# Scan layers of an audio tower: states kept in PSUM, rows spread by DMA, sums on TensorE

## The chip, the cores and the metric

The kernel runs on one core of one Trainium2 chip. The metric is the device time of one execution in microseconds. Everything is float32.

## The reference

The input `x` is 32 sequences of 750 tokens with 64 channels. Three state-space layers run one after the other; after each of the first two, pairs of neighbouring tokens are averaged (750, 375, 187 tokens). Then come a Taylor-softmax attention block and a block of 16 experts with top-2 gates, each on a layer norm and with a residual. The change touches the three scan layers alone:

```
A = -exp(A_log)                                  # 64 channels x 64 states
dbc = x @ W_dbc.T                                # per token: one delta, B (64), C (64)
delta = softplus(delta * W_dt + b_dt)            # per token and channel
dA  = exp(delta * A);  dBx = delta * x * B
h[t] = dA[t] * h[t-1] + dBx[t]                   # for each channel and state
y = sum over states of h * C  +  D * x
```

With the inputs' `A_log` (large), nearly all states decay to zero within one token. For them `h = dBx`, and their whole sum is a quadratic form of `x` times `delta * x`.

## The kernel before

Channels of two halves of the batch lie on the 128 partitions. A **unit** is 750 columns of tokens (748 in the third layer); there are 28: 16 in the first layer, 8 in the second, 4 in the third. Units are grouped in eight **phases** (`PHASES`): 4, 4, 4, 4, 4, 4, 2, 2 units. For each phase a **decision** is made from the data: the extremes of the raw delta (`extreme_rows`, eight matmuls into one pair of PSUM banks), the smallest delta, the states that are not "fast", their ranks, the matrix `mT2` of the fast states' quadratic form, and the two **slots** (`STATIC = 2`) of slow states that are scanned one after the other. `more_slots` is a branch for further ones, which these inputs do not take. Decisions of phases 1 to 6 are spread over the units q = 0, 1, 2 of the phase ahead (`chain`); those of phases 0 and 7 are made in one go (`straight`, before unit 0 and in the period of unit 24).

Each engine runs `period(n)`, a fixed order written out by hand, for n from -2 to 27, and meets the others by semaphores. Per unit:

- TensorE (PE), in calls of `wide` (one matmul of 512 columns and one of 238): `z` (raw delta on all partitions), `mixed` (the quadratic form's matrix times x), `summed` (sum over channels of a product), `weighted_b` for slots 0 and 1 (B spread over the partitions), `weighted_c` for slots 0 and 1 (C likewise): 7 wide calls.
- ScalarE (ACT): `softplus` of unit n+2 in five passes over `pairs[0]`, `decay` (exp) for each slot.
- GpSimd (POOL): `summed` and `corrected` (two adds that finish delta), `inputs` (`u = delta * x`), `pool_output` (pairs of tokens of `y0T` added), `add` for each slot (pairs of tokens added, then added to the next layer's x).
- VectorE (DVE): `load` (B times u, in place in PSUM) for 2 slots, `recur` (the scan, PSUM to SBUF) for 2 slots, `read` (state times C) for 2 slots, `product`, `by_delta`, `output`, `corrected`: 10 passes of 750.
- SyncE (SP) loads x in seven parts, then the later parameters (`later`, 15 transfers), and in the scans nothing else.

After the last unit attention and experts start; they wait for the last `add`.

## Time and profile before

| | |
|---|---|
| three runs | 847.52 us median (841.94 to 850.53) |
| profiled execution | 842.01 us, span 840.2 us, mean TensorE clock 0.959 |
| first scan starts / scans end / attention starts | 44.60 / 369.0 / 371.87 us |
| busy in the span | PE 738.7, DVE 569.5, POOL 482.3, ACT 364.2 us |

A busy PE is not PE at its peak: matmul ends are modelled. A line can be that of a helper: all wide matmuls have lines 388 and 389, and the tiles tell them apart. A record of a float32 matmul comes twice (x2). In the scans the start of one instruction to the start of the next (its **pitch**) is shorter than its duration, since neighbours overlap.

### The profile page before, as it was taken

The page shows a single profiled execution, that of the slowest core. Times are in us where ns is not written, and L with a number is a line of the kernel's source. Part 1 is how long each engine was busy: PE and PEld are TensorE (multiplying, and loading weights), DVE is VectorE, ACT ScalarE, POOL GpSimd, SP SyncE. Part 2 cuts the span into 40 slices and gives each one's busy share as a digit, 9 for nine tenths or more (in the row PEclk, how much of TensorE's full clock was granted, in tenths as well). Part 3 has the DMA queues.
Part 4 walks back from the last instruction along what each step waited for, and adds up shares of the span by engine and source line. Part 5 has one row for each costly group of instructions (what it writes and reads, how often), then busy time and mean ns, then how long its engine had stood idle before and what let it go on. Part 6 is the DMA issues. An engine that isn't in the chain of part 4 may idle for free.

```text
span 840.2 us, 10716 instructions
## 1 busy us (share of the span) xinstructions
PE 738.7 (88%) x3396; PEld 383.1 (46%) x3396; DVE 569.5 (68%) x861; ACT 364.2 (43%) x638; POOL 482.3 (57%) x508
## 2 busy tenths in 40 slices
PE   4689888998889896855998888979999999999997
PEld 2345454554545453522776666753333333333332
DVE  3199899999999997665348888848454445444443
ACT  2345555454655454312444444444344333443332
POOL 2379788988888896543555555523344434444441
PEclk9699999999999999776799999999999999999999
DMA  8200000000000000022000000063594433444400
GB/s 300 80 1 1 1 1 2 0 2 1 2 1 1 2 0 1 1 55 45 2 1 1 3 4 3 3 126 78 106 188 89 91 88 84 98 98 98 104 1 19
DMA packets 19078, 37.40 MB, mean 45 GB/s; under 512 B 2255, under 2 KB 17607, under 8 KB 18375
## 3 DMA queue, kind: packets, MB, share of 16 engines
q1 hardware_dynamic: 18711, 36.01, 18.5%
q8 instruction: 30, 0.49, 0.2%
q10 hardware_dynamic: 304, 0.63, 0.2%
q14 instruction: 33, 0.27, 0.1%
HBM read 34.72 MB, written 1.92 MB: 44 GB/s over the span
## 4 chain that ended last, share of the span: by engine, by line
PE 66%; DVE 16%; ACT 7%; issue 5%; POOL 1%; DVEq 0%; ACTq 0%; POOLq 0%
PE pair L712 21%; PE pair L388 12%; PE pair L733 10%; PE pair L389 5%; PE pair L615 5%; DVE tmp L1107 4%; PE pair L598 3%; PE pair L647 2%; ACT work L776 2%; ACT work L777 2%; DVE pair L1080 1%; PE pair L445 1%; PE pair L634 1%; PE pair L477 1%; DVE tmp L1115 1%
## 5 line engine op out<-in xcount | busy, mean ns | idle before, releaser
L1360 DVE TENSOR_TENSOR hidden<-pair,tmp 128x502 f32<-128x502 f32 (+1 forms) x192 | 121.5, 675 | 130.1 <-PE pair L712 105.2
L1520 POOL TENSOR_TENSOR hidden<-xs,big 128x502 f32<-128x502 f32 (+1 forms) x96 | 111.8, 1166 | 167.4 <-PE pair L712 146.5
L964 ACT ACTIVATE tmp<-pair 128x502 f32<-128x502 f32 (+1 forms) x192 | 102.5, 586 | 156.9 <-PE pair L712 156.9
L1544 POOL TENSOR_TENSOR big<-big 94x512 f32<-94x512 f32 (+3 forms) x120 | 89.6, 782 | 81.4 <-DVE big L1262 71.7
L712 PE MATMUL pair<-xs,w 64*128 64x502 f32 (+1 forms) x384 | 108.2, 640 | 0.5 <-DVE big L1294 0.5
L712 PE MATMUL pair<-hidden,w 64*128 64x502 f32 (+1 forms) x384 | 98.6, 589 | 1.8 <-DVE hidden L1360 1.6
L1107 DVE TENSOR_TENSOR_SCAN tmp<-tmp,pair 128x750 f32<-128x750 f32 (+1 forms) x56 | 95.5, 1705 | 0.1
L733 PE MATMUL pair<-hidden,w 128*64 128x502 f32 (+1 forms) x384 | 91.1, 596 | 0.0
L794 ACT ACTIVATE tmp<-big,picked 128x749 f32<-128x749 f32 (+2 forms) x56 | 51.1, 912 | 86.6 <-issue 49.5
L388 PE MATMUL pair<-big,work 128*128 128x512 f32 x128 | 67.5, 609 | 11.8 <-ACT work L777 3.6
L1382 POOL TENSOR_TENSOR big<-big,work 128x750 f32<-128x750 f32 (+1 forms) x28 | 45.5, 1624 | 48.5 <-ACT big L781 48.5
L388 PE MATMUL pair<-x,work 128*128 128x512 f32 x96 | 51.7, 621 | 11.9 <-DVE tmp L1115 3.9
L712 PEld LDWEIGHTS pair<-xs,w 64*128 64x128 f32 x384 | 29.6, 187 | 67.3 <-issue 36.0
L712 PEld LDWEIGHTS pair<-hidden,w 64*128 64x128 f32 x384 | 37.3, 189 | 48.8 <-issue 46.0
L1097 DVE TENSOR_TENSOR pair<-pair,big 128x750 f32<-128x750 f32 (+1 forms) x56 | 52.2, 931 | 2.2 <-issue 2.0
L1389 POOL TENSOR_TENSOR big<-big,work 128x750 f32<-128x750 f32 (+1 forms) x28 | 46.5, 1662 | 10.3 <-DVE work L1067 8.6
L1115 DVE TENSOR_TENSOR tmp<-tmp,pair 128x750 f32<-128x750 f32 (+1 forms) x56 | 51.7, 924 | 0.5 <-PE pair L389 0.4
L733 PEld LDWEIGHTS pair<-hidden,w 128*64 128x64 f32 x384 | 23.4, 136 | 61.9 <-DVE hidden L1360 34.8
L1414 POOL TENSOR_TENSOR x<-x,work 128x375 f32<-128x375 f32 (+1 forms) x48 | 43.8, 913 | 6.9
L776 ACT ACTIVATE work<-pair,packed 128x750 f32<-128x750 f32 (+1 forms) x28 | 24.8, 886 | 47.4 <-PE pair L389 47.4
L615 PEld LDWEIGHTS pair<-big 93*120 93x120 f32 (+1 forms) x384 | 42.8, 186 | 2.6 <-issue 1.4
L615 PE MATMUL pair<-big 93*120 93x65 f32 (+1 forms) x384 | 43.3, 270 | 0.0
(187 smaller groups left out, 1265.7 us busy)
## 6 DMA issues: line engine op xcount, KB each, us to landing
big<-dispatched SPq DMA_DIRECT2D x40, 502.0 KB, 6.6
big<-in_x SPq DMA_DIRECT2D x3, 1500.0 KB, 11.8
big<-dispatched SPq DMA_DIRECT2D x8, 498.0 KB, 5.8
w<-in_w SPq DMA_DIRECT2D x5, 512.0 KB, 7.1
big<-in_x SPq DMA_DIRECT2D x4, 375.0 KB, 4.0
out<-resid SPq DMA_DIRECT2D x8, 187.0 KB, 7.6
packed<-in_packed ACTq DMA_DIRECT2D x1, 424.5 KB, 4.7
dispatched<-tmp SPq DMA_DIRECT2D x8, 47.0 KB, 1.5
```

Of the source, the lines that this page charges most:

```text
L388: pe.matmul(dst[:, 0:512], lhsT, rhs[:, 0:512], start=True, stop=True)
L615: mm = pe.matmul(bank[4 + n % 2][0:FT, at:at + 65], kF[r % 2][0:rows, unit, FT * f:FT * f + FT], qkv[r % 2][0:rows, unit, 143:208], start= ...
L712: pe.matmul(dst[:, 0:hi - lo], weights[blk, HID * e:HID * e + HID], x[blk, :], start=True, stop=True)\
L733: mm = pe.matmul(bank[4][64 * b:64 * b + 64, 0:hi - lo], w3[:, e, :], hidT[(2 * expert + b) % 8][:, 0:hi - lo], start=(e == 0), stop=(e == ...
L794: act.activation(seqs(dA[j], l)[:, :, 1:], seqs(of(delta, n), l)[:, :, 1:], ACT.Exp, scale=picked[p % 2][:, j:j + 1]).then_inc(dk_a, 1)
L964: act.activation(sT[i % 4][:, 0:w], bank[BANK1[i]][:, 0:w], ACT.Silu).then_inc(silu_a, 1)
L1097: v.tensor_tensor(bu, bu, of(u, n), ALU.mult).then_inc(bu_v, 1)
L1107: v.tensor_tensor_scan(hT[j][:, 0:w], dA[j][:, 0:w], pairs[j][:, 0:w], 0.0, ALU.mult, ALU.add)\
L1115: v.tensor_tensor(h, h, pairs[2][:, 0:w], ALU.mult).then_inc(hc_v, 1)
L1360: v.tensor_tensor(hidT[i % 8][:, 0:hi - lo], bank[BANK2[i]][:, 0:hi - lo], sT[i % 4][:, 0:hi - lo], ALU.mult)\
L1520: pool.tensor_tensor(xw[e % 4][:, 0:hi - lo], xs[:, lo:hi], wx[:, e, 0:hi - lo], ALU.mult)\
L1544: ins = eng.tensor_tensor(dst[:, :, at:at + H * m].rearrange("p u (h d) -> p u h d", d=m), t[:, :, :, 0:m], t[:, :, :, k:D], ALU.mult)
```

## The change

- **States in PSUM.** `recur` scans in place over B u in `pairs[1]` and `pairs[2]`; `read` writes state times C to SBUF (`hC`, double).
- **Rows spread by DMA.** `z` and `weighted_c` go. In their place `rows(k)` makes, with four 32-column matmuls in one bank, the two slots' rows of C (unit n+1) and the raw delta's row (unit n+3); ACT copies them to SBUF (`rows_out`), and SP writes them to DRAM (4 transfers) and reads them back spread over 64 partitions each (2 transfers for delta, `St`; 2 for C, `Ct`).
- **Sums on TensorE.** `sums(n, part)` adds D x and both slots' parts for even and odd tokens in one bank: six matmuls of 375 (374) columns; ACT copies the sum to the next layer's x (`sums_out`); POOL adds the fast states' part (`add`, once a unit).
- **Softplus.** The scaling by `W_dt` is ACT's (`wdtc`); the correction, once a DVE pass, is a sixth ACT pass and one more POOL pass. ACT does `softplus` in two parts.
- `by_delta` and `output` become one DVE pass (times `u`). The decisions' POOL steps go to ACT and DVE.
- Buffers: delta and u are rings of 7 units; x parts 4 to 6 and `later` are issued between the first events.

The diff, cut:

```diff
+RING = 7
+LATE_Z = UB[NP - 1] - 2
+ROWS = {-2: [(None, 0), (None, 1)]}
+for _n in range(-1, UNITS - 1):
+    ROWS[_n] = [(_n + 1, _n + 3 if _n + 3 < UB[NP - 1] else None)]
+    if _n == LATE_Z:
+        ROWS[_n] = [(_n + 1, UB[NP - 1]), (None, UB[NP - 1] + 1)]
@@ SyncE @@
+            def spread_rows(k):
+                i, written = k % 2, 16 * sum(2 for e in EVENTS[:k + 1] for m in e if m is not None)
+                sp.wait_ge(rw_a, k + 1)
+                if k > 1:
+                    landed(k - 2)
+                for m, row, at, count in zip(EVENTS[k], (0, 4), (0, 64), (4, 2)):
+                    if m is not None:
+                        half = unit(m)[2] // 2
+                        for c in range(2):
+                            sp.dma_start(rowsd[i, row:row + count, half * c:half * c + half],
+                                         rowsT[i][at + 32 * c:at + 32 * c + count, 0:half]).then_inc(rw_d, 16)
+                sp.wait_ge(rw_d, written)
...
-            for i in range(1, 7):
+            for i in range(1, 4):
                 load(i)
-            sp.wait_ge(zeroed, 1)
-            for dst, src in later:
-                sp.dma_start(dst, src).then_inc(later_in, 16)
-            sp.wait_ge(xa_g, STATIC * UNITS)
+            for k in range(len(EVENTS)):
+                spread_rows(k)
+                if k in (1, 2, 3):
+                    load(k + 3)
+                elif k == 4:
+                    sp.wait_ge(zeroed, 1)
+                    for dst, src in later:
+                        sp.dma_start(dst, src).then_inc(later_in, 16)
+            sp.wait_ge(xa_g, UNITS)
@@ TensorE @@
+            def sums(n, part):
+                terms = [(diagD[:, l, :], x)] + [(ident, t) for t in hC[n % 2]]
+                    if part == 0:
+                        after(pe, sm_a, TAKEN[n] - 1)
+                    pe.wait_ge(hc_v, STATIC * n + part + 1)
+                    for i in ((0, 1), (2,))[part]:
+                        for k, t in enumerate(halves(terms[i][1], l)):
+                            mm = pe.matmul(parts(bank[1], l), terms[i][0], t, start=(i == 0 and k == 0),
+                                           stop=(i == 2 and k == 1))
...
              def period(n):
+                if q == 1:
+                    extremes_spread(p)
                 if here:
                     weighted_b(n, 1)
+                if q in (1, 2):
+                    pe.wait_ge(dec_v, p * DECV + (3, 8)[q - 1])
+                for k in range(EVENT_AT[n], EVENT_AT[n + 1]):
+                    rows(k)
+                old = n - 1 if n > 0 and last_of(n - 1) is None else None
...
+                if old is not None:
+                    sums(old, 0)
+                if nxt:
                     summed(n + 1)
...
+                if nxt and q != 0:
+                    weighted_b(n + 1, 0)
+                if old is not None:
+                    sums(old, 1)
+                if q == 0:
+                    pe.wait_ge(dec_v, p * DECV + 1)
+                    weighted_b(n + 1, 0)
                 if n + 2 < UNITS:
-                    z(n + 2)
+                    mixed(n + 2)
...
                 if last_of(n) is not None:
+                    sums(n, 0)
+                    sums(n, 1)
                     more_slots(last_of(n))
...
 @@ ScalarE @@
             def period(n):
+                if n >= 0:
+                    decay(n, 1)
+                if q == 1:
+                    bounds(p)
+                for k in range(EVENT_AT[n], EVENT_AT[n + 1]):
+                    rows_out(k)
+                if nxt and s is not None:
+                    decay(n + 1, 0)
+                if n + 2 < UNITS:
+                    softplus(n + 2, 0)
+                if q == 1:
+                    exponents(p)
+                if n + 2 < UNITS:
+                    softplus(n + 2, 1)
+                if old is not None:
+                    sums_out(old, 0)
+                if nxt and s is None:
+                    decay(n + 1, 0)
...
+                if s is not None:
+                    bounds(s)
...
 @@ VectorE @@
             def recur(n, j):
+                h = pairs[1 + j][:, 0:w]
+                v.tensor_tensor_scan(h, dA[j][:, 0:w], h, 0.0, ALU.mult, ALU.add).then_inc(sc_v, 1)
             def read(n, j):
+                v.wait_ge(c_d[n % 2], 32 * (n // 2 + 1))
+                v.tensor_tensor(hC[n % 2][j][:, 0:w], pairs[1 + j][:, 0:w], Ct[n % 2][:, j, 0:w], ALU.mult)
...
 @@ GpSimd @@
             def period(n):
                 if 0 <= n + 1 < UNITS:
-                    corrected(n + 1)
+                    softplus(n + 1)
+                    inputs(n + 1)
                 if n > 0:
-                    add(n - 1, 1)
+                    add(n - 1)
```

## Rows read from the trace of the kernel before

**Rows 1.** Busy time by stage: length, PE, PEld, DVE, ACT, POOL (instructions), PEclk, DMA, GB/s.

```profile
91.50:137.80 46.30, 41.20 (x146) 22.93 (x145) 43.00 (x50) 24.54 (x35) 39.33 (x41) 1.00 0.00 1
276.40:322.10 45.70, 40.64 (x138) 22.73 (x137) 42.55 (x51) 24.72 (x37) 39.88 (x41) 1.00 0.01 1
322.10:343.30 21.20, 14.98 (x51) 8.46 (x50) 12.23 (x21) 7.59 (x14) 14.28 (x16) 0.80 0.00 0
343.30:371.80 28.50, 20.59 (x59) 10.82 (x58) 24.75 (x24) 7.55 (x9) 14.83 (x9) 0.92 0.00 1
...
370.00:842.00 472.00, 431.70 (x2352) 212.80 (x2352) 260.98 (x487) 187.82 (x377) 203.42 (x221) 0.96 0.29 62
```

**Rows 2.** VectorE timeline of one unit: start us, us, engine, line, operation, [idle <-releaser].

```profile
172.88 1.70 DVE L1107 TENSOR_TENSOR_SCAN tmp<-tmp,pair 128x750 f32<-128x750 f32 x1
174.50 0.92 DVE L1097 TENSOR_TENSOR pair<-pair,big 128x750 f32<-128x750 f32 x1
175.33 0.92 DVE L1115 TENSOR_TENSOR tmp<-tmp,pair 128x750 f32<-128x750 f32 x1
...
181.11 0.94 DVE L1067 SCALAR_TENSOR_TENSOR work<-pair,work 128x750 f32<-128x750 f32 x1 [0.65 <-ACT pair L783]
182.50 0.95 DVE L1097 TENSOR_TENSOR pair<-pair,big 128x750 f32<-128x750 f32 x1 [0.45 <-issue]
...
184.20 1.70 DVE L1107 TENSOR_TENSOR_SCAN tmp<-tmp,pair 128x750 f32<-128x750 f32 x1
```

**Rows 3.** TensorE timeline, two `wide` calls in a row.

```profile
137.45 1.02 PE L388 MATMUL pair<-big,work 128*128 128x512 f32 x2
...
138.71 1.02 PE L388 MATMUL pair<-work,packed 128*128 128x512 f32 x2
```

**Rows 4.** TensorE timeline, the eight 32-column matmuls of `extreme_rows`.

```profile
189.52 1.47 PE L445 MATMUL pair<-x,w0pm 128*32 128x375 f32 x16 [0.36 <-ACT work L777]
```

**Rows 5.** Instruction groups of ACT and POOL, 91.5 to 322 us: count | busy, mean ns.

```profile
L1414 POOL TENSOR_TENSOR x<-x,work 128x375 f32<-128x375 f32 (+1 forms) x40 | 36.7, 917 | 5.7
L794 ACT ACTIVATE tmp<-big,picked 128x749 f32<-128x749 f32 (+2 forms) x40 | 36.5, 912 | 59.0 <-issue 32.9 <-DVE tmp L1107 22.1 <-DVEq L1138 4.0
...
L1382 POOL TENSOR_TENSOR big<-big,work 128x750 f32<-128x750 f32 (+1 forms) x20 | 32.6, 1630 | 14.9 <-ACT big L781 14.9
...
L1394 POOL TENSOR_TENSOR big<-big 128x750 f32<-128x750 f32 x11 | 19.9, 1809 | 0.0
...
L776 ACT ACTIVATE work<-pair,packed 128x750 f32<-128x750 f32 (+1 forms) x20 | 17.7, 887 | 26.8 <-PE pair L389 26.8
```

**Rows 6.** DMA: issue ns min/median/max; GB/s, 600 to 640 us; KB each, us to landing.

```profile
L359 SPq DMA_DIRECT2D big<-dispatched x48: 573/613/676, 553.2 to 779.1; - x48
...
GB/s 213 213 217 197 225 197 215 205 195 223 199 219 213 195 223 199 237 193 199 231 199 225 201 60 6 14 269 219 209 215 102 0 0 0 0 0 12 275 215 221
...
big<-in_x SPq DMA_DIRECT2D x3, 1500.0 KB, 11.8
...
dispatched<-tmp SPq DMA_DIRECT2D x8, 47.0 KB, 1.5
```

**Rows 7.** Timeline of the two decisions made in one go, at 21 and 332 us.

```profile
21.55 0.16 DVE L1044 TENSOR_REDUCE low<-pair 128x1 f32<-128x2 f32 x1 [0.68 <-PE pair L455]
...
332.30 0.16 DVE L1044 TENSOR_REDUCE low<-pair 128x1 f32<-128x2 f32 x1 [0.47 <-PE pair L455]
...
339.10 0.36 DVE L1060 COPY picked<-pair 128x192 f32<-128x192 f32 x1 [1.70 <-PE pair L477]
...
339.51 2.07 PE L388 MATMUL pair<-x,quad 128*128 128x512 f32 x2 [0.45 <-DVE picked L1060]
```

**Rows 8.** GpSimd timeline, the last sum of the scans.

```profile
370.13 1.63 POOL L1417 TENSOR_TENSOR resid<-resid,tmp 128x748 f32<-128x748 f32 x1 [0.97 <-DVE tmp L1115]
```

**Rows 9.** SyncE timeline, first and last of 15 issues of `later`.

```profile
9.25 0.57 SPq L337 DMA_DIRECT2D wqkv<-in_wqkv  x1
...
22.20 0.35 SPq L337 DMA_DIRECT2D w<-in_w  x1
```

More of the change, by code:

```diff
@@ L85, in program @@
         tmp = sb("tmp", [128, 3256])
-        delta = [big[:, 12000 + 3000 * i:15000 + 3000 * i] for i in range(2)]
-        u = [big[:, 18000 + 3000 * i:21000 + 3000 * i] for i in range(2)]
+        delta, u = (big[:, at:at + 750 * RING] for at in (13500, 18750))
         packed = sb("packed", [128, PACKED])
@@ L118, in program @@
         sext = sb("sext", [1, 2])
-        nz, zb, rz, dmin, dn, de, dL = (sb(f"low{i}", [128, 1]) for i in range(7))
+        nz, rz, dmin, dn, de, dL = (sb(f"low{i}", [128, 1]) for i in range(6))
         amax2 = sb("amax2", [128, NS])
@@ L476, in picks @@
+            def picks(p):
+                l = PHASES[p][0]
+                pe.wait_ge(dec_v, p * DECV + 9)
                 for i, t in enumerate((AT, wBT, wCT)):
-                    mm = pe.matmul(pairs[pair][:, NS * i:NS * i + NS], t[:, l, :], onehot[:, :], start=True, stop=True)
+                    mm = pe.matmul(bank[0][:, NS * i:NS * i + NS], t[:, l, :], onehot[:, :], start=True, stop=True)
                 mm.then_inc(dec_p, 1)
@@ L759, in _ @@
             mm.then_inc(setup_p, 1)
+            pe.wait_ge(setup_v, 2)
+            for l in range(LAYERS):
+                mm = pe.matmul(bank[4][:, l:l + 1], wdtr[0:1, l, :], ident[0:1, 0:1], start=True, stop=True)
+            mm.then_inc(setup_p, 1)
             pe.wait_ge(setup_v, SETUP_V)
+            pe.wait_ge(zeroed, 2)
             for n in range(-2, UNITS):
@@ L1151, in period @@
                     load(n, 1)
+                if q == 1:
+                    smallest_delta(p)
+                if here:
                     read(n, 0)
[L1153 to L1155 removed]
                     recur(n, 1)
+                if q == 0:
+                    extremes(p)
+                elif q == 1:
+                    classes(p)
+                elif q == 2:
+                    picks(p)
                 if nxt:
                     output(n + 1)
[L1159 to L1164 removed]
                 if here:
@@ L1375, in _, with softplus @@
             pool.sem_inc(more_g, 1)
-            def summed(n):
+            def softplus(n):
                 _, _, w, _ = unit(n)
-                d = of(delta, n)
+                d, e = of(delta, n), E[n % 2][:, 0:w]
                 pool.wait_ge(log_a, n + 1)
```

538 lines of the change are left out of this document (263 added, 275 removed).

## Prediction

> **What bounds the kernel now.** I read the busy time by stage first. The scan stage runs in phases of four units that repeat at 46 us; VectorE is busy 43.0 of 46.3, TensorE 41.2, GpSimd 39.3, ScalarE 24.5 [rows 1]. The stage from 370 us on (472 us) holds nothing that the change touches, so its cost is carried over. Then VectorE's own timeline: a scan has a pitch of 1.62 us, another pass of 750 columns 0.83 to 0.86 (I take 0.84). Ten passes are 2 x 1.62 + 8 x 0.85 = 10.0 us; the unit shown, in which no step of a decision falls on VectorE, takes 184.20 - 172.88 = 11.32, and the gaps are a wait for ScalarE (0.65) and a branch at the phase's end (0.45) [rows 2]. So VectorE sets the pace.
>
> TensorE's busy time hides how near it is. Two wide calls in a row start 1.26 us apart: 1.68 ns a column [rows 3]. Seven of them are 8.8 us a unit, 35.3 a phase. The eight 32-column matmuls of `extreme_rows` take 1.47 together [rows 4]: 3000 columns at 0.49 ns, so four column groups run at once. Busy 41.2 less 35.3 and 1.5 leaves at most 4.4 for the decision's small matmuls; records overlap, and I take 2.7. TensorE's real load is 39.5 of 46.3, with 6.8 idle.
>
> **The change, part by part**, in a phase of four units of layers 1 and 2.
>
> *VectorE* loses `corrected` and one of `by_delta`/`output`; the scan writes PSUM instead of SBUF, and no row has that. Passes in place in PSUM (0.92) and SBUF to SBUF through PSUM (0.92) cost alike [rows 2], so I take 1.62; bounds 1.5 and 1.8. Eight passes are 2 x 1.62 + 6 x 0.84 = 8.3 us: 1.7 us a unit saved, if VectorE stays the bound. The decision's steps that come over from GpSimd (a few small passes, some 1 us a phase) lie in the slack that this leaves; if VectorE were the bound they would cost that 1 us.
>
> *TensorE* loses three wide calls (-3.78). It gains `rows`, four 32-column matmuls of 375 columns in four groups, half of `extreme_rows`: 0.74. And it gains `sums`, six matmuls of 375 full-width columns: 6 x 375 x 1.68 ns = 3.78. A unit is 4 x 1.26 + 0.74 + 3.78 = 9.56 us; a phase 38.2 + 1.5 + 2.7 = 42.4, against 39.5. **TensorE becomes the bound.** Laid out by hand from `weighted_b(n, 1)` at 0: rows to 2.0, sums 0 to 4.5, `summed` to 5.8, `weighted_b(n+1, 0)` to 7.1, sums 1 to 8.3, `mixed` to 9.6. VectorE's 8.3 us fits in with some 0.8 to spare before `mixed` and `weighted_b(n+1, 1)`. The last unit of a phase carries two units' sums and the branch (13.9), q = 0 none. TensorE's stalls: q = 0 waits for the reduction of the extremes (1.1) and their row (0.35), the branch costs 0.5, q = 1 waits for `fast_weights` behind ScalarE's queue (0.6), q = 2 for the ranks (0.3): 2.8. A phase is 45.2; bounds 42.4 (no stall) and 49.2 (as much idle as now). Against 46.1 that is -0.9 a phase, -5 over the five phases to 322 us.
>
> The sums read every second token. No row shows a matmul that does; the bounds are 1.68 ns a column and twice that, +15 us a phase. GpSimd adds 375 such pairs (`add`) without any penalty, which speaks for the lower end, and I take it. The Trainium skill ("SBUF — State Buffer", the block on cachelines) says that a step of up to four fp32 is free, and no run here shows it for TensorE.
>
> *GpSimd* per unit: three passes for delta (1.63 each), `inputs` 1.81, one add in halves (0.8) and one of 0.92 [rows 5]: 8.4, under 9.6. But `add(n-1)` now waits for TensorE's sums and ScalarE's copy, and stands ahead of the next softplus. From the sums' end at 8.5: copy 0.6, add 1.0, three passes and `inputs` 6.9, `output` 0.85, then `mixed`: 2 units in 19.4 us, so 9.7 a unit. It binds about with TensorE and has no slack.
>
> *ScalarE*: six passes at a pitch of 0.8, two decays of 0.91 [rows 5], two half-width copies of 0.5: 7.6 us a unit. It stays hidden.
>
> *The DMA round trip* is new. SP issues eight transfers a unit: a small one 0.3 to 0.6, a spread one 0.61 [rows 6]. From `weighted_b` at 0: rows out at 2.8, writes issued to 4.7, landed at 5.8 (1.5 for a small one), spread reads issued to 8.3. They move 384 KB (delta) and 768 KB (C); spreads run at some 210 GB/s [rows 6], so 5.5 us and C is there at 13.3. `read(n+1, 0)` wants it at 13.5 to 14.5: hidden, by 0.2 to 1.2. If that cover is gone, each late us costs about half a us a unit. The Trainium skill ("DMA: Bandwidth & Descriptors", Anatomy of one DMA) gives 2.0 us of fixed cost, heaviest for writes to HBM; this trace's 1.5 for a small write speaks for less. By 2.0 the write lands 0.5 later and half of the cover is gone, which would speak for the second rival below.
>
> *Start.* ScalarE's `bounds` of the first decision now stands behind `softplus(0)`, which waits for a round trip: delta's minimum is known at 21.55 [rows 7], softplus ends at some 25.4, so the decision is 3.8 late. Against this, unit 1's softplus needs no z by then. I get the first scan at 43.5 to 45 (44.6 now): 0. In phase 0, x parts 5 and 6 (1500 KB each) and then `later` go between events on one queue. The 15 issues of `later` take 22.55 - 9.25 = 13.3 us [rows 9], 5.4 of it one blocked issue; with 8.3 the event of unit 3 is some 3 us late. Phase 0 would save 0.6 and loses 3 and 1.6 (first C): +4. Bounds 0 and +12.
>
> *The straight decision at unit 24.* The stage from scan 24 to scan 25 is 21.2 us at a granted clock of 0.80 [rows 1]: 10.2 to the minimum, 6.8 to the picks, then a wide call at the lower clock (2.07 for 512 columns, 1.02 elsewhere) [rows 3, 7]. After: `bounds(s)` stands behind `softplus(26, ...)`, and row 26 leaves only in this period: `weighted_b` 2.5 us behind the scan, rows and copy 2.7, writes and landing 2.8, delta spread 3.5, softplus 4.9, `bounds` 1.0: 17.4, then 6.1 to the picks. `weighted_b(25, 0)` comes behind them, ahead of `mixed`, both on a slow clock: 6.3 instead of 4.2 to the next scan. 29.8, so **+8.6**; bounds +3 and +12.
>
> *Tail* (28.5 now [rows 1]). Two units of sums, 3.8 us each, stand where VectorE has no `product` to hide them, and the last unit's come behind the last read: 3.8, copy 0.6, add 1.63 [rows 8], where only the add was. I get 33.6, **+5.1**; bounds +3 and +8.
>
> **Sum**: 0 + 4 - 5 + 8.6 + 5.1 = +12.7; I halve the first phase's +4, since C's wait overlaps the late event: +10. The profiled execution took 842.0, so 852. It is at the low end of its runs (median 847.5); I leave the forecast at **853**.
>
> **Rivals.** *Faster*: TensorE fills its gaps, a phase costs 42.8, and the straight decision loses 4 only. 5 x -3.3, -3 in phase 0, +4, +4: -11.5, about 831. For it: the decision's waits are short and TensorE's queue is in order but never starved by VectorE (8.3 under 9.6). Against: GpSimd's loop of 9.7. It decides from a phase under 44.
> *Slower by a wait*: C lands 3 us later than laid out (17 instead of 13.3), since transfers with others queued land late: 1500 KB of x took 11.8 us [rows 6], and the eight issues of an event share one queue. The loop C, read, `weighted_b(n+1, 0)`, sums 1, `mixed`, next `weighted_b` is (18.1 + 3)/2 = 10.6 a unit: +20 over the scans, 873. It decides from 1.3 us of lateness.
> *Strided sums at half rate*: +3.8 a unit, some 950.
>
> **Chances.** My layout (843 to 863) 0.52; faster rival 0.23; wait rival 0.20; strided 0.05. Within 1% (about what tells from no change here, 8.5 us): 0.36 of the first, 0.04 of the second. Slower: 0.16 of the first, and the last two. The range, 831 to 877, takes in the bounds of the phase (42.4 to 47 for most).
>
> **What would show it.** TensorE's start-to-start over a whole phase and its idle: 45 us with under 3 idle and VectorE near 37 busy of 45. `read` waiting for DMA `spread` says the round trip binds. A 375-column matmul of `sums` at 0.63 pitch; four of `rows` in 0.74. Scan 25 starting 30 us behind scan 24, with ScalarE's first bound at 17. The end of the last add 4 us later behind the last read. A phase above 47 or under 44 would prove my layout wrong.

## The result and the profile after

| | before | after |
|---|---|---|
| median of the runs shown | 847.3 us (841.9 to 850.5, 4 runs) | 873.6 us (863.8 to 875.3, 4 runs) |
| ratio, 95% interval | | 1.029 [1.020, 1.039] |
| profiled execution, span | 842.0, 840.2 us | 875.3, 873.5 us |
| first scan starts | 44.6 | 42.7 |
| attention starts | 371.9 | 398.9 |

The change made the kernel 2.9% slower. 853 had been forecast, with a range to 877; the likeliest case's own range ended at 863, so the total is that of the rival by a wait (873), though not by its mechanism: that the range still holds the result is luck. Where the scans lose their 27.1 us, by the starts of the first slot's scans (a phase is four units; all us; the column of the prediction adds up to +11.2, where its own sum rounds the five phases to -5 and the whole to +10):

| stretch | before | after | difference | predicted |
|---|---|---|---|---|
| start to first scan, and phase 0 | 44.6 + 46.9 | 42.7 + 49.0 | +0.2 | +2 |
| phases 1, 2, 3 | 46.3, 46.4, 46.0 | 46.1, 46.0, 46.1 | -0.5 | -2.7 |
| phase 4 (units 16 to 19) | 46.2 | 49.3 | +3.1 | -0.9 |
| phase 5 (units 20 to 23) | 45.7 | 48.3 | +2.6 | -0.9 |
| scan 24 to scan 25 (straight decision) | 21.2 | 34.8 | +13.6 | +8.6 |
| scan 25 to attention (tail) | 28.6 | 36.6 | +8.0 | +5.1 |

The profile after, by stage, answers to [rows 1]: length, PE, PEld, DVE, ACT, POOL (instructions), PEclk, DMA, GB/s.

```profile
42.70:91.70 49.00, 41.05 (x157) 21.03 (x158) 37.03 (x45) 32.32 (x51) 29.19 (x22) 0.97 0.67 190
91.70:137.80 46.10, 44.72 (x179) 23.41 (x178) 36.92 (x47) 32.77 (x50) 32.99 (x25) 1.00 0.40 105
229.90:279.20 49.30, 45.98 (x179) 23.63 (x178) 37.11 (x46) 32.88 (x51) 32.84 (x25) 0.97 0.38 95
279.20:327.50 48.30, 45.77 (x167) 23.87 (x166) 36.49 (x46) 32.85 (x51) 32.87 (x25) 0.96 0.35 92
327.50:362.30 34.80, 20.96 (x66) 10.38 (x65) 11.65 (x22) 11.89 (x23) 14.38 (x10) 0.71 0.18 45
362.30:398.90 36.60, 27.72 (x86) 14.01 (x85) 22.09 (x21) 13.12 (x20) 13.24 (x8) 1.00 0.18 43
398.90:873.50 474.60, 437.34 (x2352) 217.34 (x2352) 261.34 (x486) 187.70 (x377) 201.72 (x220) 0.95 0.29 61
```

In the second row VectorE fell from 43.0 to 36.9 and TensorE rose from 41.2 to 44.7 of 46.1: the bound changed hands and the pace did not move. Phases 4 and 5 have the same matmuls as that row or fewer (179 and 167), a lower granted clock, and take 3.2 and 2.2 us more. The last row is the untouched stage. Before, the same stretch reads:

```profile
371.90:840.20 468.30, 431.67 (x2352) 212.74 (x2352) 260.92 (x486) 187.82 (x377) 201.71 (x220) 0.96 0.29 62
```

The same 2352 matmuls take 5.7 us more TensorE time and the stage 6.3 more, at a mean granted clock of 0.95 instead of 0.96; the other engines' busy time agrees within 0.5 us. That is where this pair's other 6.3 us lie (with the 27.1, and but for rounding, the 33.3 between the spans). Nothing in that stage was changed, and the medians differ by 26.3 us, so I count it as the clock of these two executions and not as a cost of the change. The experiments below bear this out: none of them touches the stage, and it took from 463.5 us (clock 0.98) to 473.7 us (0.95) in their profiles. Totals of single runs can differ by 10 us from this alone, so the stages are what to compare.

**One unit after** (TensorE's timeline of unit 11; start us, us, engine, line, operation).

```profile
172.81 1.02 PE L454 MATMUL pair<-big,work 128*128 128x512 f32 x2
...
174.17 0.51 PE L476 MATMUL pair<-big,rowsel 128*32 128x375 f32 x2
...
174.93 1.59 PE L514 MATMUL pair<-big,diagD 128*128 128x375 f32 x4
...
177.68 1.02 PE L454 MATMUL pair<-work,packed 128*128 128x512 f32 x2
178.53 0.56 PE L455 MATMUL pair<-work,packed 128*128 128x238 f32 x2
178.94 1.02 PE L454 MATMUL pair<-big,work 128*128 128x512 f32 x2
...
180.20 1.50 PE L514 MATMUL pair<-tmp,packed 128*128 128x375 f32 x4
181.53 1.02 PE L454 MATMUL pair<-big,quad 128*128 128x512 f32 x2
182.39 0.57 PE L455 MATMUL pair<-big,quad 128*128 128x238 f32 x2
182.79 1.48 PE L514 MATMUL pair<-big,diagD 128*128 128x375 f32 x4
```

The order is the one laid out by hand: `weighted_b`, `rows`, `sums` part 0, `summed`, `weighted_b`, `sums` part 1, `mixed`. There is no wait in it. Start to start: 1.36 + 0.76 + 2.75 + 1.26 + 1.26 + 1.33 + 1.26 = 9.98 us, where I had 9.56. VectorE in the same stretch:

```profile
173.01 0.94 DVE L1227 TENSOR_TENSOR work<-pair,big 128x750 f32<-128x750 f32 x1 [1.14 <-PE pair L455]
173.87 1.72 DVE L1249 TENSOR_TENSOR_SCAN pair<-tmp,pair 128x750 f32<-128x750 f32 x1
175.49 0.92 DVE L1242 TENSOR_TENSOR pair<-pair,big 128x750 f32<-128x750 f32 x1
...
180.01 0.94 DVE L1235 TENSOR_TENSOR work<-pair,big 128x750 f32<-128x750 f32 x1 [1.13 <-PE pair L455]
```

Now it is VectorE that waits for TensorE. A scan in place in PSUM starts 1.62 us before the next pass, as the scan to SBUF did [rows 2].

**The new waits of phase 4.** GpSimd, then TensorE:

```profile
234.47 1.78 POOL L1536 TENSOR_TENSOR big<-big 128x750 f32<-128x750 f32 x1
...
237.10 0.98 POOL L1548 TENSOR_TENSOR big<-big,work 128x375 f32<-128x375 f32 x1
```
```profile
235.92 0.56 PE L455 MATMUL pair<-work,packed 128*128 128x238 f32 x2
238.44 2.73 PE L532 MATMUL pair<-big,w0pm 128*32 128x375 f32 x16 [1.95 <-POOLq L1572]
```

`extreme_rows` for phase 5 reads x of the second layer, whose last quarter holds the sums of units 14 and 15. GpSimd's `add(15)` stands at the end of its period, behind softplus and `inputs`, and the branch behind it. TensorE waits 1.95 us, and then the eight 32-column matmuls take 2.73 where they took 1.47 [rows 4]: the granted clock is 0.50 there (238.4 to 241.2).

**The straight decision.** TensorE, then ScalarE:

```profile
331.80 0.82 PE L476 MATMUL pair<-big,rowsel 128*32 128x374 f32 x4
335.61 0.82 PE L482 MATMUL pair<-big,w0pm 128*32 128x374 f32 x4 [2.99 <-POOL big L1548]
...
350.53 0.42 PE L547 MATMUL pair<-packed,amax 128*64 128x128 f32 x1 [6.20 <-ACT amax L907]
...
356.10 2.07 PE L454 MATMUL pair<-big,work 128*128 128x512 f32 x2 [0.45 <-DVE picked L1221]
```
```profile
343.80 1.01 ACT L868 ACTIVATE work<-spread,packed,wdtc 128x748 f32<-128x748 f32 x1 [4.20 <-DMA spread<-rowsd]
...
348.86 0.28 ACT L898 ACTIVATE low<-low,packed 128x1 f32<-128x1 f32 x1
```

Read from the end: the picks are at 355.7, 28.2 us behind scan 24 (327.5; [rows 7] for before). ScalarE's first bound starts at 348.86, right behind the softplus of unit 26, which waited 4.20 for delta's rows by DMA. Those rows left late, since the matmuls for them (L482) waited 2.99 us for a late `add` again, that of unit 23. All the while the delta's minimum, all that the bound needs, was there at 344.5.

**The tail** (TensorE, the last unit):

```profile
391.71 0.87 PE L522 MATMUL pair<-big,diagD 128*128 128x374 f32 x2 [1.64 <-DVE work L1259]
392.42 1.42 PE L522 MATMUL pair<-work,packed 128*128 128x374 f32 x4
394.41 0.90 PE L522 MATMUL pair<-big,diagD 128*128 128x374 f32 x2 [0.57 <-ACT resid L937]
395.14 1.42 PE L522 MATMUL pair<-work,packed 128*128 128x374 f32 x4
398.96 1.59 PE L653 MATMUL pair<-resid,centering 128*128 128x376 f32 x2 [2.39 <-POOL resid L1551]
```

Behind the last read (its end: 391.57) stand two halves of three matmuls in one bank, with ScalarE's copy between them (0.57 wait), the second copy (396.60) and the add (397.22 to 398.85): 7.3 us. In the third layer the change takes the sum in two parts that share `bank[1]`.

### The profile page after: what moved, and what is told of

Same layout as the page of the kernel before. It is cut to its first block, busy times and chain, and to the rows that moved or that the text cites. A ratio compares the mean times of both kernels' runs of the same rounds, so it can differ in the third digit from the quotient of the medians.

```text
span 873.5 us, 11316 instructions
## 1 busy us (share of the span) xinstructions
PE 778.2 (89%) x3626; PEld 393.0 (45%) x3626; DVE 529.6 (61%) x841; ACT 426.2 (49%) x753; POOL 435.1 (50%) x399
## 3 DMA queue, kind: packets, MB, share of 16 engines
q1 hardware_dynamic: 28855, 68.76, 32.4%
## 4 chain that ended last, share of the span: by engine, by line
PE 44%; DVE 7%; ACT 2%; issue 1%; POOL 0%; POOLq 0%; DVEq 0%; ACTq 0%
PE pair L798 20%; PE pair L819 10%; PE pair L701 5%; PE pair L684 3%; PE pair L733 2%; PE pair L720 1%; DVE big L1341 1%; PE pair L748 1%; PE pair L742 1%; PE pair L665 1%; PE pair L522 0%; DVE big L1346 0%; DVE big L1359 0%; DVE big L1636 0%; ACT big L1057 0%
## 5 line engine op out<-in xcount | busy, mean ns | idle before, releaser
L1249 DVE TENSOR_TENSOR_SCAN pair<-tmp,pair 128x750 f32<-128x750 f32 (+1 forms) x56 | 95.8, 1710 | 1.2 <-ACT tmp L892 1.1
L454 PE MATMUL pair<-big,work 128*128 128x512 f32 x112 | 61.2, 628 | 11.6 <-DVE smx L1184 5.3
L1548 POOL TENSOR_TENSOR big<-big,work 128x375 f32<-128x375 f32 (+1 forms) x24 | 22.0, 915 | 81.2 <-ACT big L937 80.7
L819 PEld LDWEIGHTS pair<-hidden,w 128*64 128x64 f32 x384 | 23.4, 136 | 61.9 <-DVE hidden L1504 34.8
L701 PEld LDWEIGHTS pair<-big 93*120 93x120 f32 (+1 forms) x384 | 47.1, 202 | 3.3 <-issue 2.2
L1536 POOL TENSOR_TENSOR big<-big 128x750 f32<-128x750 f32 (+1 forms) x28 | 46.6, 1665 | 2.2
L701 PE MATMUL pair<-big 93*120 93x65 f32 (+1 forms) x384 | 47.4, 285 | 0.0
L1531 POOL TENSOR_TENSOR big<-big,work 128x750 f32<-128x750 f32 (+1 forms) x28 | 46.2, 1649 | 2.2
L1529 POOL TENSOR_TENSOR work<-work 128x750 f32<-128x750 f32 (+1 forms) x28 | 46.3, 1652 | 0.8 <-ACT work L881 0.8
L733 PE MATMUL pair<-big 120*64 120x188 f32 x384 | 37.4, 347 | 1.9 <-issue 1.2
```

The lines of the kernel that those rows point to most:

```text
L454: pe.matmul(dst[:, 0:512], lhsT, rhs[:, 0:512], start=True, stop=True)
L701: mm = pe.matmul(bank[4 + n % 2][0:FT, at:at + 65], kF[r % 2][0:rows, unit, FT * f:FT * f + FT], qkv[r % 2][0:rows, unit, 143:208], start= ...
L733: mm = pe.matmul(dst[64 * b:64 * b + 64, TOK * k:TOK * k + TOK], kvm[n % 2][:, k, FTN * b + f, :], qT[n % 2][:, f, TOK * b:TOK * b + TOK], ...
L819: mm = pe.matmul(bank[4][64 * b:64 * b + 64, 0:hi - lo], w3[:, e, :], hidT[(2 * expert + b) % 8][:, 0:hi - lo], start=(e == 0), stop=(e == ...
L1249: v.tensor_tensor_scan(h, dA[j][:, 0:w], h, 0.0, ALU.mult, ALU.add).then_inc(sc_v, 1)
```

## The experiments

Each is an edit of the changed kernel. Stages are again those of the table; a single profiled run each, if nothing else is said. Beside them the kernel before took 842.2, 847.0 and 842.9 us. Three of the kernels leave the straight decision as the change has it (`later` moved, x by ScalarE, the tail): it took 34.1, 34.0 and 34.1 us there, so 0.7 of the change's 34.8 belongs to its one profile.

**TensorE as the bound.** One term of the sums is left out.

```diff
-                    for i in ((0, 1), (2,))[part]:
+                    for i in ((1,), (2,))[part]:
```

> TensorE leaves D x out of its sums: 2 of 6 matmuls of 375 columns fewer in each unit; what is computed lacks D x. Theory 1 (TensorE is the bound of the middle units, back to back): a unit loses 1.3 to 1.4 us as long as nothing else binds, a phase of the first layer goes from 46.1 to 41 to 42. Rival A (the loop sums, copy, GpSimd's add, its three passes, output, mixed, 9.7 us a unit): the phase stays above 44. Rival B (DMA round trip): above 44 with VectorE waiting for DMA.

Phases 1 to 3 took 42.0, 42.0, 41.7 (46.1, 46.0, 46.1 in the change); 851.4 us in all. By stage, phase 1:

```profile
93.70:135.70 42.00, 39.92 (x163) 20.17 (x162) 36.54 (x46) 32.54 (x50) 33.68 (x26) 1.00 0.43 109
```

Two matmuls of 375 columns less a unit are 8 x 0.66 = 5.3 us a phase by the pitches above; 4.1 came back. TensorE does set the pace of the middle stages, and the next limit is 1.2 us behind it.

**The same work on VectorE**: D x as a second pass there (a multiply by delta, then D added and times x), four matmuls of sums.

```diff
-                v.tensor_tensor(y0T[n % 3][:, 0:w], pairs[3][:, 0:w], of(u, n), ALU.mult).then_inc(y_v, 1)
+                v.tensor_tensor(pairs[3][:, 0:w], pairs[3][:, 0:w], of(delta, n), ALU.mult).then_inc(t_v, 1)
...
+                v.scalar_tensor_tensor(y0T[n % 3][:, 0:w], pairs[3][:, 0:w], dskip[:, l:l + 1], x, ALU.add, ALU.mult)\
+                    .then_inc(y_v, 1)
```

> D x goes back from TensorE's sums to VectorE (by_delta and output as two passes, as before the change); TensorE keeps four matmuls of 375 columns a unit. Theory 1 (TensorE binds, VectorE has 9 of 46 us a phase free): TensorE sheds 1.35 us a unit, VectorE gains 0.86 and is at 9.2 of then about 10.4; a phase of the first layer goes from 46.1 to 42 to 43.5, phases 5 and 6 shrink by 2 to 4 us as well, straight and tail by 1 to 3: 18 to 28 us less up to attention. Rival (VectorE or GpSimd's loop binds at once): 44.5 or more a phase.

Phases 1 to 3: 45.1, 45.1, 45.3; 871.1 us in all. Its longest waits in phase 1 (us in total, times, longest):

```profile
PE pair L454 <- DVE work L1237: 3.2, 4, 1.0
```

TensorE's load fell about as much as in the run before (40.5 us busy, 39.9 there), but `mixed` of the next unit now waits up to 1.0 us for VectorE's longer `output` (the queue on the one buffer `pairs[3]`). The change's exchange of passes for matmuls is worth minus one us a phase here: neither engine alone is the limit at 45. The total hides it, since phases 4 and 5 took 49.9 and 47.2 at clocks of 0.93 and 0.96 and the untouched stage 473.7.

**GpSimd's load**: one of its passes for delta left out.

```diff
-                pool.tensor_tensor(e, e, W[:, 0:w], ALU.subtract).then_inc(cor_g, 1)
...
+                pool.tensor_tensor(d, d, W[:, 0:w], ALU.add).then_inc(dl_g, 1)
```

> GpSimd leaves out one of its three passes for delta (the correction is added without its subtraction, so delta is not exact). Theory 1 (TensorE binds): phases of the first layer stay at 46.1 within 0.3. Rival (GpSimd's loop binds or nearly binds): 0.5 to 1.5 us less a phase. At the joints of phases 5 and 6 and before the straight decision the add comes 1.6 us sooner, so 1 to 2 us less each by the theory of the late add.

Phases 1 to 3 stayed (46.1, 46.1, 46.0), so GpSimd's loop does not bind there. Phases 4 and 5 fell from 49.3 and 48.3 to 46.5 and 45.2, the straight decision from 34.8 to 32.4: 855.8 us in all. That points at one late step of GpSimd and not at its load. Part of it is the clock, which was 1.00 in both phases.

**The late `add`, moved to the front** of GpSimd's period in units 15, 19 and 23:

```diff
+                first = n - 1 in (15, 19, 23)
+                if first:
+                    add(n - 1)
+                    more_slots(last_of(n - 1))
                 if 0 <= n + 1 < UNITS:
                     softplus(n + 1)
                     inputs(n + 1)
-                if n > 0:
+                if n > 0 and not first:
```

> GpSimd adds the last unit of a phase (and runs the phase's branch) ahead of the next softplus, for units 15, 19 and 23 alone. Theory 1 (TensorE's extreme_rows and the raw-delta rows wait for GpSimd's late add, because the wait names the whole source phase): phases 5 and 6 shrink from 49.3 and 48.3 us by 1 to 3 us each (the softplus that now comes later gives back about 1), the 3.0 us wait before L482 at 335.6 goes, so the straight decision shrinks from 34.8 to about 32; in all 5 to 8 us less up to the start of attention. Rival (the second layer is dearer because of the DMA spreads or the clock): phases 5 and 6 stay within 0.5 us.

869.4 us; phases 4 and 5 took 50.2 and 51.1, and only the straight decision gained (31.6). TensorE was busy 46.3 and 47.1 us in the two, against 44.8 and 44.1 at full clock (next experiment), so 1.5 and 3.0 of it is the clock. VectorE in phase 4:

```profile
242.09 0.94 DVE L1235 TENSOR_TENSOR work<-pair,big 128x750 f32<-128x750 f32 x1 [3.02 <-POOL big L1536]
```

`extreme_rows` is in time, but `add` waits for TensorE's sums and ScalarE's copy at the front of the queue, and `inputs` behind it comes late: `output` waits 3.02 us for `u`. The wait has only moved: less the clock's part, an estimate, the phases are 48.7 and 48.1, no shorter than the 48.1 and 46.6 with the add left late.

**The late `add` in the middle**, between softplus and `inputs`:

```diff
             def inputs(n):
+                if n - 2 in (15, 19, 23):
+                    add(n - 2)
+                    more_slots(last_of(n - 2))
                 pool.wait_ge(dl_g, n + 1)
```

> GpSimd adds units 15, 19 and 23 between the softplus and the inputs of the next unit but one: 1.8 us sooner than in the change, with the softplus not delayed. Theory 1 (late add; the version with the add first moved the wait to VectorE's output, which waited 3.0 us for GpSimd's inputs): phases 5 and 6 go from 49.3 and 48.3 to 46.5 and 45.5, as in the version with a pass less (46.5, 45.2), the straight decision from 34.8 to about 33. Rival (what helped there was a shorter GpSimd queue): within 1 us of the change.

859.6 us; phases 4 and 5 took 46.2 and 45.3, the straight decision 32.7 (2.1 less than in the change's profile, 1.3 less than in the three kernels that leave it alone). The two stages beside those of a kernel with the add left late (the one below in which ScalarE issues x), both at full clock; first the add in the middle, then late:

```profile
230.40:276.60 46.20, 44.72 (x178) 23.46 (x177) 37.11 (x46) 32.88 (x51) 32.88 (x25) 1.00 0.41 102
276.60:321.90 45.30, 44.06 (x167) 23.15 (x166) 36.39 (x46) 32.86 (x51) 32.88 (x25) 1.00 0.38 98
```
```profile
230.10:278.20 48.10, 44.77 (x178) 23.46 (x177) 37.15 (x46) 32.89 (x51) 32.90 (x25) 1.00 0.38 99
278.20:324.80 46.60, 44.06 (x167) 23.12 (x166) 36.47 (x46) 32.86 (x51) 32.86 (x25) 1.00 0.36 94
```

Every engine's busy time is the same; the add's place costs 1.9 and 1.3 us. The change's own profile has 1.2 and 1.7 more in these stages at clocks of 0.97 and 0.96, with 1.2 and 1.7 more TensorE busy time: that part is the clock. So +5.7 of phases 4 and 5 is 3.2 for the wait, 2.9 for the clock and -0.4 for the rest.

**The bounds ahead of the softplus** in the decisions made in one go, on ScalarE:

```diff
                 if nxt and s is not None:
                     decay(n + 1, 0)
+                if s is not None:
+                    bounds(s)
+                    exponents(s)
+                    fast_weights(s)
+                    spread_weights(s)
                 if n + 2 < UNITS:
                     softplus(n + 2, 0)
```

> In the two decisions made in one go ScalarE computes bounds, exponents, weights and the spread of the weights before the softplus that waits for the DMA. Theory 1 (the decision stood behind that softplus): from the minimum of delta to the picks 11.3 us become about 7, scan 24 to scan 25 from 34.8 to 30 to 31 us, the first scan within 2 us of before (softplus now comes later there). If the late softplus of unit 26 is the next to end last, 2 to 4 us of this come back in the tail of 36.6. Rival (the slow clock and TensorE's chain set the decision): under 1 us.

865.5 us; the straight decision fell to 30.8 (-4.0; -3.3 against the three kernels that leave it alone). Phase 4, which the edit does not touch, took 50.9 at a clock of 0.93. ScalarE:

```profile
346.62 0.29 ACT L898 ACTIVATE low<-low,packed 128x1 f32<-128x1 f32 x1 [5.37 <-DVE low L1196]
```

The bound now waits for delta's minimum itself, as it should. At the other straight decision, ahead of unit 0, the first scan started at 44.8 and not at 42.7, and phase 0 took 46.9 and not 49.0; the sum is the same 91.7. The start and phase 0 are one stretch whose end something else sets (next).

**What sets phase 0.** First, `later` (15 transfers) is moved from behind event 4 to behind event 24.

```diff
-                elif k == 4:
+                elif k == 24:
```

> The 15 transfers of later are issued after the 25th event instead of the fifth. Theory 1 (in phase 0 the rows of unit 3 stand on SP's queue behind them): phase 0 goes from 49.0 to 46 to 47, the rest unchanged. Rival (phase 0 is dearer through the x parts or the first C): 48.5 or more. If 15 issues late in the scans hold an event up there, the straight decision or the tail grows by up to 5 us.

Phase 0 took 48.6 (49.0), 864.1 us in all. That looks like nothing, but unit by unit it is two differences of opposite sign. VectorE at unit 3, in the change and then with `later` moved:

```profile
85.68 0.94 DVE L1259 TENSOR_TENSOR work<-pair,spread 128x750 f32<-128x750 f32 x1 [4.97 <-DMA spread<-rowsd]
```
```profile
81.70 1.72 DVE L1249 TENSOR_TENSOR_SCAN pair<-tmp,pair 128x750 f32<-128x750 f32 x1
...
91.68 1.72 DVE L1249 TENSOR_TENSOR_SCAN pair<-tmp,pair 128x750 f32<-128x750 f32 x1
```

In the change the first `read` of unit 3 waits 4.97 us for its C, whose rows were written behind `later` (its last issue at 73.47, the write at 73.97), and the unit takes 13.6 us from its scan (78.17) to the next. With `later` moved the wait is gone and the unit takes 9.98: -3.6. Unit 0 took 16.6 us there and 13.4 in the change: +3.2, at a granted clock of 0.69 and not 0.87, and with 1.0 us more of waiting for the first C. Unit 0 took as long (16.1, 17.2 and 17.4) in three kernels that leave `later` in its place (add in the middle, x by ScalarE, the tail), so the move of `later` is not what made it long.

Then x parts 5 and 6 are issued by ScalarE, on its own queue, and not by SyncE between the events:

```diff
-                if k in (1, 2, 3):
+                if k == 1:
                     load(k + 3)
...
+                if n in (0, 1):
+                    lo, hi = X_PARTS[n + 5]
...
+                    act.dma_start(big[:, X_AT[0] + lo:X_AT[0] + hi], a["x"][:, g, at:at + hi - lo])\
+                        .then_inc(x_in[n + 5], 16)
```

> The change, with x parts 5 and 6 issued by ScalarE at the start of its periods 0 and 1, and not by SyncE behind events 2 and 3. The bytes and their time are nearly the same; only the queue is another. Queue theory (the prediction's: an event's small writes stand behind 1500 KB of x on the one queue): the reads of the events that now follow 6.1 and 5.6 us behind the first write (44.00 to 50.10, 57.72 to 63.27) follow in some 2.8 us as in the middle of the scans; the first four scans' phase (49.0 now) falls by 1.5 to 3, to 46 to 47.5. Rival 1 (the 16 DMA engines are shared whatever the queue is): the gaps stay over 5 us and the phase at 49. Rival 2 (the phase is long from its low clock at 47 to 50 us and from the first C alone, 1.0): the gaps fall but the phase stays within 0.6 of 49.0.

Phase 0 took 49.2, 864.7 us in all. SyncE's issues (writes of rows L374, reads of them L381):

```profile
44.04 1.18 SPq L374 DMA_DIRECT2D rowsd<-rows  x4
50.92 1.09 SPq L381 DMA_DIRECT2D spread<-rowsd  x2
...
61.55 1.18 SPq L374 DMA_DIRECT2D rowsd<-rows  x4
63.65 1.09 SPq L381 DMA_DIRECT2D spread<-rowsd  x2
```

The second event no longer stands behind x (2.1 us from the first write to the read, 5.6 in the change), the first one still does (6.9): another queue does not help while 1500 KB are in flight. That the second is free is no gain of the queue either: it left 13.3 us behind the issue of x part 6 (48.27), which lands in some 9.4, and with x on SyncE's queue but 8.0 us ahead of it the same event took 2.4 (run before, 61.25 to 63.66). Of my account of phase 0 the late event is shown, at 3.6 us; that the queue as such blocks is not. The C behind `later` also sets the end of the stretch in most runs: the first `read` of unit 3 starts at 85.7 in the change and at 85.2 to 87.1 in six others with `later` in its place (add first and in the middle, a pass less on GpSimd, x by ScalarE, the tail, the repairs together), however early or late their first scan, and the next phase starts 6.1 behind it. With the bounds first it started at 84.0, and a wide call at the low clock (1.90 us at 85.07) made the rest 7.7.

**The DMA round trip's cover**: C is spread twice a unit, one after the other.

```diff
+                                     rowsd[i:i + 1, 2 * b:2 * b + 2, 0:w].to_broadcast([64, STATIC, w]))\
+                            .then_inc(c2_d, 16)
+                    sp.wait_ge(c2_d, 32 * (c_of + 1))
+                    for b in range(2):
```

> The spread of C is done twice for each unit, the second after the first has landed; only the second counts. It makes C 5 to 6 us later and doubles its bytes, results are the same. Theory 1 (the DMA round trip is hidden in the change, with about 1 us to spare): each unit now waits, VectorE's read for DMA, by (5.5 - 1)/2 or more, so a phase of the first layer goes from 46.1 to 54 to 62. If the cover were much larger than thought, under 2 us a phase; if the round trip had bound already, at least 11 us a phase more.

954.6 us; phases 1 to 4 took 57.5 to 58.3, phase 5 55.9. VectorE's waits for it (us in total, times, longest), 91 to 230 us:

```profile
DVE work L1265 <- DMA spread<-rowsd: 30.0, 5, 10.4
```

In the change VectorE never waits for `spread` in phases 1 to 3. With C some 5.5 us later (375 KB land in 5.2 to 5.7) a unit takes 2.9 us more, half a us for each: the price that the prediction named, if there is next to no cover. But TensorE's clock was down too (0.91 in phase 1, 1.1 us a unit more busy), so what the delay alone costs lies between 1.7 and 2.9. An estimate from the change's own trace: the second transfer of unit 11's C was issued at about 168.5 (the pair: 167.84 to 169.08) and lands in 5.7, so by 174.2, and its first `read` starts at 176.32, so the cover is about 2 us. It is real and it is small.

**The tail**: the last unit's two parts in two banks, D x and slot 0 ahead of the last read.

```diff
+                elif n == UNITS - 1:
...
+                            for half in range(2):
+                                mm = pe.matmul(bank[1 - half][:, 0:374], terms[i][0],
+                                               terms[i][1][:, 374 * half:374 * half + 374],
+                                               start=(i == 0), stop=(i == 2))
```

> The change, with the last unit's sums in two banks: D x and slot 0 for both halves stand ahead of the wait for the last read, and only slot 1's two matmuls (1.3 us) behind it, with the two copies behind them, the second overlapping none of TensorE. Nothing is left out. My theory of the tail: from the last read's end to the start of attention there are now 5.5 us of sums and copies (391.6 to 397.1) before the last add of 1.63; they become 1.3 + two copies of 0.5 = 2.4, so the tail (36.6 us from scan 25 to the attention) falls by 3, to 33.6, which would be the value that I had predicted by other terms. Rival: the tail is long from the low clock and the C rows' late landing ahead of the last reads (0.65 wait), and the end of the sums is covered by the attention's own start: the tail falls by under 1.

869.3 us; the tail took 34.8 (-1.9), between the two expectations. TensorE:

```profile
388.40 1.53 PE L528 MATMUL pair<-big,diagD 128*128 128x374 f32 x4 [0.57 <-ACT resid L953]
389.76 2.68 PE L528 MATMUL pair<-work,packed 128*128 128x374 f32 x8
```

The ping-pong is gone from the last unit. But its first matmul starts only at 388.40, held by the copy of the unit before, so little of D x and slot 0 was ahead of the last read (its end: 389.2).

**The repairs together**: add in the middle, bounds first, tail.

> The change with three repairs together: GpSimd's add of units 15, 19 and 23 in the middle of its period (1.9 + 1.3 us by the phases 48.1 and 46.6 at full clock against 46.2 and 45.3), ScalarE's bounds ahead of the next softplus in the decisions made in one go (4.0), and the last unit's sums in two banks (1.9). If the repairs add up: first 43 to 44.5, then 49.5, 46.1, 46.1, 46.1, 46.2, 45.3, a straight decision of 29 to 30 and a tail of 34.7, so the attention starts at 386 to 388 (398.9 in the change, 371.8 before). With the rest at 468 to 474 us the total is 856 to 863, 1 to 2% over before and 1.5% under the change. Rival: the straight decision's two gains are one (the decision waits for GpSimd's branch and for ScalarE in parallel): it stays at 31 to 33, the total at 860 to 867.

860.0 us median (851.2 to 862.3, 5 runs), ratio to before 1.018 [1.014, 1.023]. In its profiled run (851.2) attention started at 383.0, phases 4 and 5 took 46.2 and 45.3, the tail 35.1 and the straight decision 27.0, shorter than the 28.7 that the two gains taken from 34.8 leave. Its stage, answering to the 34.80 above:

```profile
320.90:347.80 26.90, 19.16 (x65) 9.81 (x64) 11.31 (x22) 11.10 (x23) 9.48 (x7) 0.81 0.21 59
```

Phase 0 took 46.6 with the first scan at 44.7. And with D x on VectorE beside them:

> The same, with D x back on VectorE as in e6_dx_vector: two passes there, four matmuls of sums on TensorE. With one engine's load moved to the other, a phase of the first layer took 45.1 instead of 46.1. If that holds beside the repairs: three phases 1 us shorter, the layer-1 phases 45.2 and 44.3, the tail 1 us shorter: the attention starts at 381 to 383, total 850 to 857; it would still be 1% slower than before, since the straight decision (29 against 21) and the tail (34 against 28.6) are not paid back. Rival: with VectorE's chain output to mixed on the path, the repairs give less, as in e6 where the phases 4 and 5 kept 49.9 and 47.2: no gain over e13.

853.5 us median (852.3 to 855.8, 4 runs), ratio to before 1.011 [1.006, 1.015]. Phases 1 to 3 took 45.1, 45.1, 45.3, the straight decision 28.7, the tail 34.1; attention started at 381.0. It is the best version tried, and it is still 1.1% slower than the kernel before. Of the 6.5 us between the two medians the start of attention explains 2.0 (381.0 against 383.0). The rest is not explained: the two profiled runs differ the other way (855.8 against 851.2), by the untouched stage (472.9 against 466.3).

## Why the prediction came out as it did

**TensorE becomes the bound: right**, by its load (44.7 of 46.1) and by the run without D x. Mis-sized was the unit, 9.98 us and not 9.56. The sums are a count of columns by 1.68 ns in the prediction, 0.63 a matmul; they measured 0.66 to 0.69 (2.75 for four, 1.33 for two), and `weighted_b` ahead of the 32-column matmuls 1.36 and not 1.26. `rows` took 0.76 (0.74 predicted). That is 0.42 a unit, 1.7 a phase; a phase came out 0.9 longer than predicted, 46.1 and not 45.2, since the decision's stalls were less than the 2.8 that I gave them (TensorE is idle 1.4 in all). So phases 1 to 3 gained 0.5 and not 2.7, and of the mark "45 us with under 3 idle" the length was missed by a us, while the idle time and "VectorE near 37" were met.

**Strided sums at half rate: rightly set aside, but the step is not quite free.** L514 reads every second token and L522 in the third layer a contiguous row; the groups (count | busy, mean ns of one | idle), first 91.7 to 327.5 us, then the tail:

```profile
L514 PE MATMUL pair<-tmp,packed 128*128 128x375 f32 x48 | 17.8, 493 | 0.0
```
```profile
L522 PE MATMUL pair<-tmp,packed 128*128 128x374 f32 x16 | 5.7, 477 | 0.0
```

493 against 477 ns for each of a matmul's two records. Start to start, two matmuls ahead of a wide call take 1.33 us strided (180.20 to 181.53) and 1.26 contiguous (376.03 to 377.29 in the tail): 0.66 against 0.63, so it is the step and not the matmul's shape that is over the count of columns. That is 5% and not double, and the rival at 950 us falls. By the Trainium skill ("SBUF — State Buffer", the block on cachelines) a step of up to four fp32 is free; this trace has 0.03 us a matmul for a step of two, 0.2 of the 0.42 us a unit above.

**The round trip is hidden: right**, and its price of half a us for each us late was near (0.3 to 0.5 by the run with C twice). The rival of C landing 3 us late (873 us) has the measured total, but by another mechanism: no `read` waited in phases 1 to 3. (In phase 0 they waited 7.2 us in all, 5.0 of it behind `later`, and in the tail 0.65.) The small writes were no dearer than the 1.5 us that I took: SyncE's four were issued in 1.18 us and had landed 2.1 us behind the first one's issue (164.60, the read's issue at 166.71). The 2.0 us that the prediction quotes from the Trainium skill ("DMA: Bandwidth & Descriptors", Anatomy of one DMA) are stated there for transfers issued by GpSimd, and these are SyncE's. Landing of the spreads, KB each and median us:

```profile
spread<-rowsd SPq DMA_DIRECT2D x48, 375.0 KB, 5.7
spread<-rowsd SPq DMA_DIRECT2D x48, 187.5 KB, 3.3
```

**GpSimd binds about with TensorE: wrong as a loop, right as a place.** That `add(n-1)` "stands ahead of the next softplus" was the danger that I named; the loop had slack. What I did not follow was who else waits for the end of `add` and the branch behind it: `extreme_rows` of the next phase (`x_ready`), and the raw-delta rows of the straight decision. In the first layer x comes from the input and nobody waits, which is why phases 1 to 3 show nothing. Price: 1.9 + 1.3 in phases 4 and 5, and of the straight decision 1.3 to 2.1 alone or 3.8 on top of the bounds' move (30.8 to 27.0, at clocks of 0.67 and 0.81).

**The straight decision: the mechanism right, the size not** (+8.6 predicted, +13.6). The bounds did stand behind softplus(26) and its round trip, but ScalarE's first bound came 21.3 us behind scan 24, where the terms add up to 16.4. The step that failed is "`weighted_b` 2.5 us behind the scan, rows and copy 2.7": SyncE's write was to start 5.2 behind the scan and started 9.5 behind it (336.98). Of these 4.3 us, 2.99 are the wait for GpSimd. The steps behind it were near: from the first write to the delta spread's landing 6.8 (6.3 predicted), softplus 5.1 (4.9), picks to the next scan 6.6 (6.3). With both causes mended the stretch is 27.0; the last 5.8 over before are not taken apart. Its clock is 0.81 against 0.71 in the change and 0.80 before, so part of the repair's gain may be the clock's; and 0.7 of the +13.6 is the one profile's, by the three kernels at 34.0 to 34.1.

**The tail: the mechanism right, the size not** (+5.1, +8.0). The last unit's sums took 4.85 us (391.71 to 396.56, 0.57 of it a wait), and those of a unit inside the tail 4.61 to the next other work (372.68 to 377.29), where I had 3.8. That is the shared bank, which the prediction's sum left out. (Of its +5.1 the terms named give 4.4, sums 3.8 and copy 0.6; it names no row for the other 0.7.) Two banks for the last unit gave back 1.9 of the 2.9 that were missing; the other 1.0 is not taken apart.

**Phase 0 +4, halved: right in the late event and in the sum; the start 0: wrong** (together +0.2 against +2). Phase 0 came out 2.1 longer, and the late event of unit 3 costs 3.6 of it where I had 3. The first scan came 1.9 us earlier, where I had no change. As the C behind `later` holds the end of the stretch, an earlier start gains nothing: the edits of the decision's order moved the border between the two and not their end. How much phase 0 would gain with `later` out of the way is not shown, since unit 0 was slower in the run that has it; with the change's unit 0 it would be 3.6, an estimate.

**The total.** Of +27.1 up to attention, 3.2 is the wait of phases 4 and 5, 13.6 and 8.0 the two straight-line stretches, and 2.9 the clock in phases 4 and 5; the rest is -0.6. The prediction had the two stretches at 13.7 together (21.6 measured) and the five phases at -4.5 (+5.2 measured): errors of 7.9 and 9.7 the same way, less 1.8 of the start and phase 0. So the sum went wrong in three places: the phases behind the first layer's end were priced like the others, with nothing for the wait of `extreme_rows` for GpSimd's last `add` (3.2) or for the clock behind it (2.9); the rows of the straight decision were to be written 5.2 us behind the scan and were written 9.5 behind it (2.99 of the difference the same wait); and the sums of the last layer, two parts in one bank, were sized without the copy between them. The 6.3 behind the start of attention belongs to the one profiled pair.

## What to carry to other kernels

A change that trades one engine's passes for another's must be costed first where steps follow each other without overlap: the three steady phases gave -0.5 us, the two such stretches +21.6. For each step put behind a later producer, list all who wait for what it signals, in the next phase too, and not only its successor on its own engine. Front, middle and end of an in-order queue are three different prices (48.1, 45.3 and 46.6 us for one phase at full clock, the first worked out). And where an edit leaves a phase's length as it was, look at its units before calling the cause refuted: -3.6 and +3.2 us hid each other in phase 0.

## What the runs showed of the hardware

- A matmul of 375 columns in float32 with 128 x 128 weights that reads every second element went at 0.66 us start to start; one of 374 in a row went at 0.63, the columns' share of the wide calls (1.68 ns each [rows 3]). A wide call ahead of 32-column matmuls took 1.36 and not 1.26.
- The granted clock fell after short waits. The eight matmuls of `extreme_rows` behind a wait of 1.95 us took 2.73 us at a granted clock of 0.50 (1.2 GHz), with the same shape 1.47 before [rows 4]; two phases with equal work ran 1.2 and 1.7 us longer at 0.97 and 0.96. With the same wait (1.96 us with x by ScalarE, 1.97 with `later` moved) they took 1.47 and the phase's clock was 1.00, so the fall is not certain.
- A small write issued 3 us behind a load of 1500 KB held up the read behind it for 6.1 us with the load on the same queue and for 6.9 with it on ScalarE's. With the load 8.0 us ahead on the same queue it was 2.4, with 13.3 us on the other 2.1, and 2.1 with no load in flight.
- The same 2352 matmuls of an untouched stage took 463.5 to 474.6 us in fourteen kernels' profiles, in step with granted clocks of 0.98 to 0.95.
